# A normalisation over images moves into the program section of the stages behind it, and two weight roundings move ahead of it

## The reference

```python
q, k, v = conv3x3(x, Wq), conv3x3(x, Wk), conv3x3(x, Wv)
att = softmax(einsum('nchw,mchw->nmhw', q, k) / sqrt(C), axis=1)   # over images, per pixel
virt = einsum('nmhw,mchw->nchw', att, v)
mu = mean(virt, axis=(1, 2, 3)); var = var(virt, axis=(1, 2, 3))   # one pair for each image
virt = (virt - mu) * rsqrt(var + 1e-05) * gamma + beta             # gamma, beta for each channel
x = x + conv3x3(relu(virt), Wc)
t = tokens(x)                                                      # 16 x 256 tokens of 128
t = t + attention(ln(t))                                           # 8 search heads, 2 retrievals
t = t + experts(ln(t))                                             # top 2 of 8, 128 -> 512 -> 128
```

## Time and profile before

| | us |
|---|---|
| three timed runs | 798.56, 800.57, 800.8 |
| their median | 800.57 |
| the profiled execution | 799.37 |
| its span, first instruction to last | 797.6 |
| mean granted TensorE clock | 0.902 of full speed |

### The profile page before, as it was taken

The page is one execution under the profiler, slowest core; times in us unless marked ns, Lnnn a source line. Parts: engine busy times, 40 slices in busy tenths (PEclk is TensorE's granted clock), DMA queues, the critical chain, the costliest instruction groups (busy, mean ns, idle before and its releaser), DMA issues. The chain is left out here.

```text
span 797.6 us, 11835 instructions
## 1 busy us (share of the span) xinstructions
PE 668.2 (84%) x3761; PEld 559.7 (70%) x3761; DVE 443.0 (56%) x1216; ACT 309.8 (39%) x616; POOL 248.4 (31%) x280
## 2 busy tenths in 40 slices
PE   5999999993788999998989897878416999999940
PEld 4888888882567889896878787877314777777730
DVE  4233333336455768685758577564422666666635
ACT  5111111110543545352534344333204777777820
POOL 2100553001820000032221313031660366666670
PEclk9999999996696999999989899797756999999985
DMA  9999772000033140313040403100137766666208
GB/s 333 317 356 350 249 243 92 0 0 0 1 113 121 31 132 16 118 46 116 8 153 1 157 4 125 35 28 0 39 113 234 231 215 220 222 220 220 101 9 316
DMA packets 56372, 105.42 MB, mean 132 GB/s; under 512 B 8872, under 2 KB 21817, under 8 KB 56192
## 3 DMA queue, kind: packets, MB, share of 16 engines
q1 hardware_dynamic: 51328, 96.24, 36.8%
q0 software_dynamic: 4992, 8.54, 3.0%
HBM read 58.15 MB, written 48.42 MB: 134 GB/s over the span
## 5 line engine op out<-in xcount | busy, mean ns | idle before, releaser
L1320 PE MATMUL bank<-rvx,s_expd 128*128 128x96 f32 x1024 | 140.3, 285 | 11.3 <-issue 10.8
L1320 PEld LDWEIGHTS bank<-rvx,s_expd 128*128 128x128 f32 x1024 | 133.6, 203 | 14.3 <-issue 12.0
L1588 POOL DMA_INDIRECT y_slots<-virt,pad_l x92 | 100.5, 1093 | 76.7 <-DVE virt L1639 50.3
L825 ACT ACTIVATE s_expd<-bank 128x512 f32<-128x512 f32 x128 | 75.7, 598 | 116.4 <-PE bank L1304 93.5
L996 DVE TENSOR_REDUCE s_max<-bank 128x2 f32<-128x512 f32 x128 | 87.5, 688 | 57.6 <-PE bank L1283 42.5
L53 PE MATMUL bank<-pad_h,w_h 128*128 (+1 forms) x216 | 88.6, 410 | 8.1 <-DVE pad_l L322 8.1
L744 POOL DMA_INDIRECT x_slots<-rows,slot_of x64 | 62.9, 983 | 78.7 <-DVE rows L1124 61.4
L54 PE MATMUL bank<-pad_l,w_h 128*128 (+1 forms) x216 | 86.2, 399 | 0.0
L55 PE MATMUL bank<-pad_h,w_l 128*128 (+1 forms) x216 | 86.2, 399 | 0.0
L713 POOL TENSOR_TENSOR ln_rstd<-ln_var,power 128x4 f32<-128x4 f32 x16 | 16.4, 1022 | 199.6 <-DVE ln_var L972 199.6
L1627 DVE TENSOR_TENSOR k_stack<-virt,k_stack 128x512 fp32r<-128x512 f32 x92 | 62.3, 686 | 18.0 <-issue 10.1
(11 more groups left out here) (238 smaller groups left out, 1255.6 us busy)
## 6 DMA issues: line engine op xcount, KB each, us to landing
x_slots<-blank SPq DMA_DIRECT2D x8, 2112.0 KB, 20.7
pad_h<-w_split SPq DMA_DIRECT2D x23, 512.0 KB
q_stack<-w_split SPq DMA_DIRECT2D x23, 512.0 KB
qk_rows<-qk SPq DMA_DIRECT2D x16, 512.0 KB
k_stack<-qk_rows SPq DMA_DIRECT2D x96, 64.0 KB, 2.2
q_stack<-qk_rows SPq DMA_DIRECT2D x48, 128.0 KB, 2.4
pad_l<-x_slots SPq DMA_DIRECT2D x23, 264.0 KB, 2.7
e_raw<-in_w SPq DMA_DIRECT2D x16, 256.0 KB, 3.4
```

The source lines that it names most:

```text
L825: nc.scalar.activation(expd[:, s % 2].rearrange("p a i -> p (a i)"), ps_st[s % 2][:, :], ACT.Exp).then_inc(exp_done, 1)
L1320: last = pe.matmul(ps_pv[s // 4][:, at:at + RVW], expd[:, s % 2, a, i * P:(i + 1) * P], rvx[:, ring, 2 * b + a, :], start=(a == 0), stop=( ...
L1588: pool.indirect_dma_start(out=y_slots[:, :], out_offset=bass.IndirectOffsetOnAxis(ap=ids, axis=0), in_=y_rows[:, t % 2, j, :], in_offset=N ...
```

## The change

`image_norm` no longer opens a section of its own. It takes the block of the last section as an argument and adds its instructions to that, ahead of those of `token_attention`; the barrier between them is gone. What the barrier ordered is now ordered by two semaphores that `image_norm` returns: ScalarE waits for the seventh step of the norm before its first image, and TensorE waits for the four border memsets before the folding matmul. `stats` and the norm's small tensors stay allocated to the end. And ScalarE rounds `wq_h` and `wk_h` ahead of that wait, not behind the fourth image. Arithmetic and instructions are otherwise the same. The body of `image_norm` is only indented differently; lines behind it move by -1 or -2, or by +1 from L1430 on (`norm_b` is written at L496 of the new code, the `k_stack` memset is L708).

```diff
-def image_norm(nc, sb, sem, bank, pad_h, pad_l, stats, gb, ones, power, norm_a, norm_b):
-    with ExitStack() as ctx:
...
-        block = ctx.enter_context(nc.Block())
...
+def image_norm(nc, ctx, block, sb, sem, bank, pad_h, pad_l, stats, gb, ones, power, norm_a, norm_b):
...
+    return b_steps, border2_zeroed
...
             for n in (2 * pair, 2 * pair + 1):
                 high(n)
 
+        nc.scalar.activation(wq_h[:, :], wq[:, :], ACT.Copy, scale=float(D) ** -0.5).then_inc(wa_high, 1)
+        nc.scalar.activation(wk_h[:, :], wk[:, :], ACT.Copy).then_inc(wa_high, 1)
+        act.wait_ge(norm_steps, 7)
         image_pair(0)
         image_pair(1)
-        nc.scalar.activation(wq_h[:, :], wq[:, :], ACT.Copy, scale=float(D) ** -0.5).then_inc(wa_high, 1)
-        nc.scalar.activation(wk_h[:, :], wk[:, :], ACT.Copy).then_inc(wa_high, 1)
         for pair in range(2, 6):
             image_pair(pair)
...
+        pe.wait_ge(border_zeroed, 4)
         pe.matmul(ps_x[:, 0:P], wqr_t[:, :], ret_blocks[:, :], start=True, stop=True).then_inc(folded, 1)
...
-            image_norm(nc, sb, sem, bank, pad_h, pad_l, stats, gb, ones, power, norm_a, norm_b)
-        with ExitStack() as late:
             block = late.enter_context(nc.Block())
+            norm_steps, border_zeroed = image_norm(nc, late, block, sb, sem, bank, pad_h, pad_l, stats, gb, ones, power,
+                                                   norm_a, norm_b)
             q_stack, k_stack = token_attention(
```

More of the change, by code:

```diff
@@ new lines, in image_norm, with _ @@
+def image_norm(nc, ctx, block, sb, sem, bank, pad_h, pad_l, stats, gb, ones, power, norm_a, norm_b):
+    chan = sb("chan", [P, NI, 2], where=ctx)
+    off = sb("off", [P, NI], where=ctx)
+    spread = sb("spread", [P, NI], where=ctx)
+    mu = sb("mu", [P, NI], where=ctx)
+    var = sb("var", [P, NI], where=ctx)
+    border2_zeroed = sem("border2_zeroed")
+    chan_done = sem("chan_done")
+    mean_summed = sem("mean_summed")
+    b_steps = sem("b_steps")
+    var_summed = sem("var_summed")
+    rstd_done = sem("rstd_done")
+    @block.gpsimd
+    def _(pool):
+        for pad in (pad_h, pad_l):
+            grid = pad[:, :].rearrange("p (n h w) -> p n h w", n=NI, h=PAD)
+            pool.memset(f32(grid[:, :, 0:PAD:PAD - 1, :]), 0.0).then_inc(border2_zeroed, 1)
+            pool.memset(f32(grid[:, :, 1:PAD - 1, 0:PAD:PAD - 1]), 0.0).then_inc(border2_zeroed, 1)
+        pool.wait_ge(b_steps, 4)
+        pool.tensor_tensor(norm_a[:, :], var[:, :], power[:, :], ALU.pow).then_inc(rstd_done, 1)
+    @block.vector
+    def _(dve):
+        for n in range(NI):
+            nc.vector.bn_aggr(chan[:, n, :], stats[:, n].rearrange("p c s -> p (c s)")).then_inc(chan_done, 1)
+        dve.wait_ge(mean_summed, 1)
+        nc.vector.tensor_copy(mu[:, :], bank[0][:, 0:NI]).then_inc(b_steps, 1)
+        dve.wait_ge(b_steps, 1)
+        nc.vector.tensor_tensor(off[:, :], chan[:, :, 0], mu[:, :], ALU.subtract).then_inc(b_steps, 1)
+        dve.wait_ge(b_steps, 2)
+        nc.vector.tensor_tensor(spread[:, :], off[:, :], off[:, :], ALU.mult).then_inc(b_steps, 1)
+        dve.wait_ge(b_steps, 3)
+        nc.vector.tensor_tensor(off[:, :], spread[:, :], chan[:, :, 1], ALU.add).then_inc(var_summed, 1)
+        dve.wait_ge(var_summed, 2)
+        nc.vector.tensor_scalar(var[:, :], bank[1][:, 0:NI], EPS, None, ALU.add).then_inc(b_steps, 1)
+        dve.wait_ge(rstd_done, 1)
+        nc.vector.tensor_scalar(norm_a[:, :], norm_a[:, :], gb[:, 0:1], None, ALU.mult).then_inc(b_steps, 1)
+        dve.wait_ge(b_steps, 5)
+        nc.vector.tensor_tensor(off[:, :], mu[:, :], norm_a[:, :], ALU.mult).then_inc(b_steps, 1)
+        dve.wait_ge(b_steps, 6)
+        nc.vector.tensor_scalar(norm_b[:, :], off[:, :], -1.0, gb[:, 1:2], ALU.mult, ALU.add).then_inc(b_steps, 1)
+    @block.tensor
+    def _(pe):
+        pe.wait_ge(chan_done, NI)
+        pe.matmul(bank[0][:, 0:NI], ones[:, :], chan[:, :, 0], start=True, stop=True).then_inc(mean_summed, 1)
+        pe.wait_ge(var_summed, 1)
+        pe.matmul(bank[1][:, 0:NI], ones[:, :], off[:, :], start=True, stop=True).then_inc(var_summed, 1)
+    return b_steps, border2_zeroed
@@ L508, in token_attention @@
 def token_attention(nc, ctx, block, sb, sem, bank, pad_h, pad_l, resid, virt, ident, wc_h, wc_l, norm_a, norm_b, power, wq, wk,
                     wvr, wqr_t, ret_blocks, wout, wg, qk_rows, consts, tile_list, out, x_slots, scattered,
-                    listed):
+                    listed, norm_steps, border_zeroed):
     S, D = 8, 16
@@ L1759, in mixed_kernel @@
                       (wqr_t[:, :], wqrT), (wout[:, :], wout_d), (wg[:, :], wg_d)]
-        with ExitStack() as early:
-            stats = sb("stats", [P, NI, NCH, 6], where=early)
+        with ExitStack() as late:
+            stats = sb("stats", [P, NI, NCH, 6], where=late)
             conv_attention(nc, sb, sem, bank, pad_h, pad_l, resid, virt, ident, wc_h, wc_l, x_chwn, x_cnhw,
```

3 lines of the change are left out of this document (2 added, 1 removed).

## The result

The changed kernel took 809.05 us in the median (807.77, 808.55, 809.55, 810.84), the kernel before beside it 800.13 (798.56 to 800.8). The ratio is 1.0116, with a 95% interval of 1.009 to 1.0142: slower, by 8.9 us. The forecast was 806.4 with a range up to 808.2, so the direction held and the time lies above the range. The profiled execution took 808.55 us, with a span of 806.8 against 797.6.

A forecast was written before the change was run, and what follows sets the result against it. The norm's chain of small steps, which all other work waits for, bounds this stretch. One hold of `norm_b` by `k_stack`, barrier gain included, adds 6.43: 799.37 to 805.8, with half the median's offset 806.4 us; range 799.3 to 808.2.

The forecast's parts named there:

- The barrier's gain: Between norm and first image: without the barrier ScalarE would start at 203.92 instead of 204.19, gain 0.27 us.
- The weights and the folding matmul: ScalarE's two weight roundings (0.40 us) and TensorE's folding matmul move ahead of the norm's end: slack only, sum 0.
- When `rvx` starts: GpSimd behind the power: the memset of `rvx` starts at about 203.08, before the power's end at 203.14.
- the first rival: Norm steps not held, by their kind or because `rvx` starts later: only 0.27 us gained, 799.7 us; chance 0.20.
- The steps are of the held kind: L494 and L498, tensor_scalar within SBUF, wait for a running GpSimd memset like the copy at L945; 6.43 us later altogether.
- The held step "gets in before the next one": A held VectorE step ends 0.02 to 0.03 us behind the running GpSimd instruction, before the next: `norm_a` about 0.45 us.
- The rival that priced the other reading: GpSimd keeps the memory across its queue, L494 waits for `k_stack` until 210.58: 806.3 or 809.7 us; chance 0.08.
- `norm_b` and the two-row memset: If L494 is held until 210.58, L498 asks near the two-row memset at 210.89: unheld 806.3, held 3.5 us more, 809.7.
- The copy at L945 meets the four-row memset: VectorE's copy, shifted to 214.8, meets the four-row memset until 217.98; its reader comes at 224.0, so cost 0.
- The clock: TensorE's low clock over the first 4.9 us of convolution: taken as 0, with 1 us either way for the range.
- The median's 0.6 us above the profiled execution: Timed runs' median lies 1.2 us above the profiled execution; half was added, 805.8 to 806.4 us.

The follow-up runs named there:

- the kernel in which GpSimd waits: Changed kernel, but GpSimd waits for the seventh norm step (`norm_b`) before its memset of `rvx`: 796.07 us against 797.53, ratio 0.9993.
- the kernel with the gap: Changed kernel, but GpSimd waits for its own memsets of `rvx` and `rows` before that of `k_stack`: 806.0 us against 797.53, ratio 1.0117.

## Why the prediction was right or wrong

*The barrier's gain*, 0.27 us: right. 0.26 us, in the kernel in which GpSimd waits.

*The weights and the folding matmul*, 0: right, by the same kernel; and the weights are worth 0 only because they stand ahead of the wait in a merged section. Alone, behind the barrier, they cost 0.40 us.

*When `rvx` starts*: forecast 0.06 us ahead of the power's end; measured 0.03 ahead (201.94 against 201.97, in rounded digits). Within the 0.1 us that decided the first rival, so this side of the point was right.

*The steps are of the held kind*: right. Both tensor_scalars were held, two-tensor forms not. This was the open question at which the row of L978 with its source in PSUM and the row with its source in SBUF disagreed; the SBUF row was the one to follow. The Trainium skill's rule ("SBUF — State Buffer", SBUF: two separate sides), weighed there, is borne out as to which pair of instructions exclude each other. As to the length, that page says the lock lasts for the whole instruction, and 7.68 us over four queued instructions is more: the measurement decides.

*The held step "gets in before the next one"*: **this is the step that failed.** It rested on one cast between two GpSimd copies, and on the copy that had ended with `k_stack`'s memset although `m_split`'s was queued behind it. Both happened; the second in the kernel before itself came out the other way when it was run again. `norm_a` was to be in and out behind `rvx` (0.45 us) and was passed over there, behind `rows` and behind `k_stack`. Its hold took 7.68 us, where the forecast had one long hold, 6.7 us, and that on `norm_b`. In neither row were more than two instructions queued behind the one that held, so neither said what a longer queue does. The rival that priced the other reading (held across the queue: 0.08) gave 809.7, a shift of 10.3 us over the profile before, where 10.27 was measured. With two rows for a behaviour and none against it, the forecast took it as the rule and gave the other reading 0.08 against 0.70.

*`norm_b` and the two-row memset*: the same rival had this, as one of two outcomes. It let the first hold end with `k_stack`, and `norm_b` then asks 0.07 us ahead of the two-row memset; measured, the hold went on through `m_split`, 0.28 us longer, and that puts `norm_b` behind that memset's start. Its number does not show this, since the memset's end sets the time. `norm_b` asks 0.22 us after that memset has started and is held 3.3 us, though the memset writes two partitions of 128. So the error is this sum: the forecast had `norm_b` stand 10.38 us behind the power's start (210.58 - 200.20). Measured, `norm_a` ended at 10.66 (209.69 - 199.03), 0.28 later than that, with `m_split` and not with `k_stack`; 0.24 more until `norm_b` asks; 3.32 for its hold. Together 3.84 us, and 6.43 + 3.84 = 10.27. The total misses by less, 808.55 against the 805.8 of the profile's scale, only because the first section was 1.17 us shorter in that execution; that is luck.

*The copy at L945 meets the four-row memset*: the mechanism is right (3.20 us in the kernel with the gap), but in the changed kernel the shift was so long that the four-row memset had ended at 216.78 and the copy ran unheld at 217.48, 0.17 us. Nothing waited for it either way.

*The clock*, 0: right here. The low level lasted 5.1 us behind the first matmul before (the forecast read 4.9) and 4.7 after (rises at 211.5 and 220.2), and the rest of the span is 0.1 us apart. The margin of 1 us either way was narrow: the rest differs by up to 7.3 us among the profiles of one chip.

*The median's 0.6 us above the profiled execution*: 0.5 was measured, 809.05 against 808.55.

## What to carry to other kernels

A barrier between sections can be doing more than ordering data: here it kept GpSimd's long memsets away from a chain of small VectorE instructions within SBUF. Before one is removed, list what each engine has queued behind it, not only what waited at it. If such memsets must run beside such a chain, write its steps as operations on two tensors, or let GpSimd wait for the chain's last step: either took the whole loss away (for the two-tensor form this is shown for memsets alone). And a hold is to be costed up to the next stop of the other engine's queue, not up to the end of its instruction: of 33 ends of a memset with another right behind, only 5 let the held instruction in.

## What was not expected of the hardware

- A held VectorE instruction waited through four, and in one kernel seven, consecutive GpSimd memsets (7.68 and 7.80 us). A stop of some 50 ns in GpSimd's queue, made by a wait for its own memsets just before, let it in.
- A memset of two partitions holds as one of 128 does: `norm_b` asked 0.22 us after its start and took 3.32 us, to its end; one of four partitions held the copy for 3.20 us.
- The same program, with VectorE asking at the same place of the memset, once got in at its end (3.29 us) and once did not (3.55 us).
- Splitting one long memset in four (1.8 us each) did not shorten the hold: 7.80 us in place of 7.68.
